# First attention layer: dense matmuls moved into the four gaps behind the attention products, turned inputs and values in one turn of a PSUM bank, two residual buffers

## The reference, cut to what matters

```
x = x + layernorm(attn(layernorm(x)))            # first layer
  attn(x): q, k, v = split(x @ w_qkv.T + b_qkv)  # x (16, 256, 128); 16 heads of 8
           a = softmax(q @ k.T / sqrt(128))      # per sequence and head, 256 x 256
           return (a @ v) @ w_o.T + b_o + x
x = x + layernorm(ffn(layernorm(x)))             # second attention, then 8 experts
```

## Time and profile before

| | us |
|---|---|
| median of 3 runs | 684.3 |
| lowest and highest | 680.41 and 688.04 |
| the profiled execution's own time | 679.28 |
| its span in the trace | 677.5 |
| mean granted TensorE clock over the span | 0.889 of 2.4 GHz |

### The profile page before, as it was taken

One profiled execution on the slowest core, in us unless ns is written; L12 is line 12 of the kernel. 1 busy time (PEld: TensorE's weight loads), 2 busy tenths in 40 slices (PEclk: granted clock), 3 DMA queues, 4 the chain that ended last, 5 costly groups with the idle time before them and its releaser, 6 DMA issues. The chain is left out here.

```text
span 677.5 us, 16101 instructions
## 1 busy us (share of the span) xinstructions
PE 552.5 (82%) x5228; PEld 415.3 (61%) x5228; DVE 455.5 (67%) x1285; ACT 373.1 (55%) x989; POOL 326.6 (48%) x543
## 2 busy tenths in 40 slices
PE   3899999999998988999991788897987409999920
PEld 2576566666665655565650677786876308999920
DVE  2366777787776667676853488888687633788870
ACT  0225666666665635665560498886774005677750
POOL 5142233334454345432114536775888750257776
PEclk9999999999998867998996699999876558999975
DMA  4200423110000000000011000000000122234333
GB/s 120 50 2 15 146 64 51 22 22 18 19 16 6 18 17 3 16 19 18 18 34 31 31 2 2 1 1 2 14 24 19 40 85 66 50 51 65 37 31 31
DMA packets 38099, 21.62 MB, mean 32 GB/s; under 512 B 13433, under 2 KB 36353, under 8 KB 38018
## 3 DMA queue, kind: packets, MB, share of 16 engines
q1 hardware_dynamic: 18544, 10.65, 7.0%
q0 software_dynamic: 6640, 4.92, 5.2%
q10 hardware_dynamic: 12834, 5.04, 3.0%
HBM read 10.11 MB, written 8.12 MB: 27 GB/s over the span
## 5 line engine op out<-in xcount | busy, mean ns | idle before, releaser
L330 DVE TENSOR_REDUCE nmax<-psA 128x2 f32<-128x512 f32 x256 | 165.3, 686 | 89.4 <-PE psA L209 89.0
L492 ACT ACTIVATE pr<-psB 128x512 f32<-128x512 f32 x250 | 136.0, 596 | 123.9 <-PE psB L226 121.4
L209 PE MATMUL psA<-km,qp 24*128 24x256 f32 x768 | 139.6, 446 | 1.0 <-POOL km L585 0.5
L226 PE MATMUL psB<-q,km 26*128 26x256 f32 (+1 forms) x752 | 118.9, 434 | 0.8 <-DMA q<-mT 0.8
L209 PEld LDWEIGHTS psA<-km,qp 24*128 24x128 f32 x768 | 91.0, 209 | 33.7 <-DVE nmax L330 23.2
L1601 POOL DMA_INDIRECT out<-wz,ys x39 | 63.5, 1627 | 53.2 <-ACT wz L1556 44.4
L585 POOL TENSOR_TENSOR km<-kraw,rows_of 128x768 f32<-128x768 f32 x16 | 23.5, 1467 | 127.7 <-ACT kraw L467 120.2
L226 PEld LDWEIGHTS psB<-q,km 26*128 26x128 f32 (+1 forms) x752 | 73.4, 202 | 1.8 <-DMA q<-mT 1.2
L240 PE MATMUL psO<-pr,v 128*32 128x256 f32 x1024 | 71.9, 401 | 0.1
L1164 ACT ACTIVATE prob<-psS,nbias 128x128 f32<-128x128 f32 x128 | 45.5, 380 | 10.4 <-DVE nbias L983 10.3
L240 PEld LDWEIGHTS psO<-pr,v 128*32 128x32 f32 x1024 | 27.5, 112 | 34.6 <-issue 23.3
(11 more groups left out here) (198 smaller groups left out, 1223.4 us busy)
## 6 DMA issues: line engine op xcount, KB each, us to landing
q<-mT SPq DMA_DIRECT2D x256, 1.0 KB
ys<-y_sorted SPq DMA_DIRECT2D x39, 72.0 KB, 1.9
e_w<-W ACTq DMA_DIRECT2D x1, 2048.0 KB
e_w<-W ACTq DMA_DIRECT2D x4, 512.0 KB
xs<-x_all SPq DMA_DIRECT2D x16, 128.0 KB
out<-x_all SPq DMA_DIRECT2D x15, 128.0 KB, 3.7
x_all<-x SPq DMA_DIRECT2D x1, 1536.0 KB, 9.1
out<-wz,ys POOLq DMA_INDIRECT x39, 3.4
```

The lines of the kernel that those rows point to most:

```text
L209: last = T.matmul(psA[:, (16 * b + n) % 3, c * L1:(c + 1) * L1], query_part(b, h, depth, c), keys(b, h, depth, slice(0, L1)), start=True, ...
L226: last = T.matmul(bank_of(b, h)[:, c * L1:(c + 1) * L1], keys(b, h, depth, slice(c * P, (c + 1) * P)), queries(b, h, depth, slice(0, L1)), ...
L330: V.tensor_reduce(nmax[:, b % 2, hf, :, at], psA[:, (16 * b + n) % 3, :].rearrange("p (c m) -> p c m", c=2), AX.X, ALU.max, negate=True).t ...
L492: A.activation(pr[:, h % PRING, :, :].rearrange("p c l -> p (c l)"), bank_of(b, h), ACT.Exp, scale=SCALE1).then_inc(S["b_free"], 1)
```

## The change

On TensorE `prep_x(i+2)` and `prep_v(i)` now follow each other in step 1, behind `attend`. `prep_qk` moves from steps 2 and 4 to 3 and 5 (behind `attend`), `project` from 6 to 7 (behind `attend`). So steps 0 and 1, 2 and 3, 4 and 5, 6 and 7 stand side by side without a full-array matmul between them. For most blocks the turned inputs of block i+2 and the values of block i share one turn of `misc` (left and right half), with one `full` and one `free`. The values are made in the block's own iteration, no longer in the one before.

`r1` has two buffers. `residual(b)` runs at the head of VectorE's iteration b+2, and waits only for the block before last on GpSimd; its statistics follow in step 1. `stats_x` moves to step 5, `normalise(i-1, 1)` to 3, `normalise(i, 0)` to 7 behind the last maxima. On ScalarE the turned inputs and the values are copied at the head of step 2, the queries at the head of 4, the keys at the head of 6, and the second order of the queries after the exponentials of step 7.

```diff
--- before.py
+++ after.py
@@ -76,7 +76,7 @@
         on = sb("on", [P, 8, 4, C1])
         onR = sb("onR", [P, L1])
         onT = sb("onT", [P, L1])
-        r1 = sb("r1", [P, 2, P])
+        r1 = sb("r1", [P, 2, 2, P])
         nr = sb("nr", [P, 2, P])
 
         psA = pb("psA", [P, 3, 512])
@@ -87,7 +87,7 @@
         names = ["ld_w", "ld_wo", "ld_b", "ld_v", "ld_x0", "ld_x1", "ld_x2", "ld_x3", "consts", "brow0", "w_zero",
                  "m_step", "w_ok", "stats0", "stats1", "aggr0", "aggr1", "ln0_step", "ln1_step", "xn_ok", "xnb_ok",
                  "full", "free", "q_ok", "k_ok", "km_ok", "v_ok", "v_zero", "a_full", "a_free",
-                 "turned", "norm_ok", "heads_ok", "onT_ok", "mrow0", "mrow1", "b_full", "b_free", "av_done", "o_ev", "rden_ok", "x1_ok", "stored",
+                 "turned", "norm_ok", "heads_ok", "onT_ok", "xnT_ok", "mrow0", "mrow1", "b_full", "b_free", "av_done", "o_ev", "rden_ok", "x1_ok", "stored",
                  "part_ok", "bias_ok"]
         S = {n: sem(n) for n in names}
 
@@ -98,6 +98,10 @@
 
             return 0 <= i + d <= LAST
 
+        def shares(b):
+
+            return 4 <= b <= LAST
+
         def piece(b):
             return next(k for k, (lo, hi) in enumerate(pieces) if lo <= b < hi)
 
@@ -105,7 +109,7 @@
 
         def turn(*name):
 
-            turns[name] = len(turns)
+            turns[name] = len(set(turns.values()))
 
         turn("w")
         turn("bias")
@@ -113,9 +117,11 @@
             for what in ("xT", "q", "k", "v"):
                 turn(what, b)
         for i in range(LAST + 2):
-            for what, b in (("xT", i + 2), ("q", i + 2), ("k", i + 2), ("out", i - 1), ("v", i + 1)):
+            for what, b in (("xT", i + 2), ("v", i), ("q", i + 2), ("k", i + 2), ("out", i - 1)):
                 if 0 <= b <= LAST and (what, b) not in turns:
                     turn(what, b)
+                if what == "v" and 2 <= i and i + 2 <= LAST:
+                    turns[("v", i)] = turns[("xT", i + 2)]
 
         def place(h):
 
@@ -174,7 +180,8 @@
                 pe.wait_ge(S["xn_ok"], b + 1)
                 for c in range(2):
                     last = T.transpose(misc[:, c * P:(c + 1) * P], xn[:, b % 2, c, :], ident[:, :])
-                last.then_inc(S["full"], 1)
+                if not shares(b):
+                    last.then_inc(S["full"], 1)
 
             def prep_qk(b, k, t):
                 if t == 0:
@@ -185,16 +192,16 @@
                 if t == 1:
                     made.then_inc(S["full"], 1)
 
-            def token_major(lhs, k):
-
-                for c in range(2):
-                    last = T.matmul(misc[:, c * P:(c + 1) * P], lhs[:, c * P:(c + 1) * P], wvo[:, k, :],
+            def token_major(lhs, k, half=0):
+
+                for c in range(2 * half, 2 * half + 2):
+                    last = T.matmul(misc[:, c * P:(c + 1) * P], lhs[:, c % 2 * P:(c % 2 + 1) * P], wvo[:, k, :],
                                     start=True, stop=True)
                 last.then_inc(S["full"], 1)
 
             def prep_v(b):
                 begin("v", b)
-                token_major(xnT[:, b % 2, :], 0)
+                token_major(xnT[:, b % 2, :], 0, int(shares(b + 2)))
 
             def scores_for_max(b, n):
 
@@ -265,13 +272,13 @@
                         attend(i - 1, 3)
                     if g == 1 and fits(i, 2):
                         prep_x(i + 2)
-                    if g in (2, 4) and fits(i, 2):
+                    if g == 1 and i >= 2 and here:
+                        prep_v(i)
+                    if g in (3, 5) and fits(i, 2):
                         prep_qk(i + 2, g // 2 - 1, 0)
                         prep_qk(i + 2, g // 2 - 1, 1)
-                    if g == 6 and done:
+                    if g == 7 and done:
                         project(i - 1)
-                    if g == 7 and i >= 1 and next_:
-                        prep_v(i + 1)
 
             pe.wait_ge(S["w_ok"], 5)
             prep_x(0)
@@ -313,13 +320,14 @@
             def residual(b):
                 dve.wait_ge(S["full"], turns[("out", b)] + 1)
                 dve.wait_ge(S["xnb_ok"], b + 1)
-                dve.wait_ge(S["x1_ok"], b)
-                V.tensor_tensor(out=r1[:, :, :], in0=misc[:, 0:2 * P].rearrange("p (c d) -> p c d", c=2),
+                dve.wait_ge(S["x1_ok"], count(b - 1))
+                V.tensor_tensor(out=r1[:, b % 2, :, :], in0=misc[:, 0:2 * P].rearrange("p (c d) -> p c d", c=2),
                                 in1=xnb_all[:, 2 * b:2 * b + 2, :], op=ALU.add).then_inc(S["free"], 1)
 
             def residual_stats(b):
                 dve.wait_ge(S["free"], turns[("out", b)] + 1)
-                ln_stats(1, b, r1, mv_r)
+                dve.wait_ge(S["x1_ok"], b)
+                ln_stats(1, b, r1[:, b % 2, :, :], mv_r)
 
             def maxima(b, n):
                 h = n ^ 2
@@ -365,6 +373,8 @@
             def iteration(i):
                 next_, done = fits(i, 1), fits(i, -1)
                 for g in range(8):
+                    if g == 0 and fits(i, -2):
+                        residual(i - 2)
                     if g == 2 and done:
                         turn_rows(i - 1, 1)
                     if g == 6 and fits(i, 0):
@@ -374,18 +384,15 @@
                         maxima(i + 1, 2 * g + 1)
                     if g in (3, 7) and next_:
                         turn_maxima(i + 1, g // 4)
-                    if g == 0 and fits(i, -2):
+                    if g == 1 and fits(i, -2):
                         residual_stats(i - 2)
-                    if g == 1 and fits(i, EARLY):
+                    if g == 5 and fits(i, EARLY):
                         stats_x(i + EARLY)
-                    if g == 2 and done:
+                    if g == 3 and done:
                         normalise(i - 1, 1)
-                    if g == 3 and done:
                         heads(i - 1)
-                    if g == 6 and fits(i, 0):
+                    if g == 7 and fits(i, 0):
                         normalise(i, 0)
-                    if g == 7 and done:
-                        residual(i - 1)
 
             stats_x(0)
             dve.wait_ge(S["w_zero"], 1)
@@ -438,7 +445,11 @@
                 if b >= 2:
                     ready("v", b - 2)
                 ready("xT", b)
-                A.activation(xnT[:, b % 2, :], misc[:, 0:L1], ACT.Copy).then_inc(S["free"], 1)
+                last = A.activation(xnT[:, b % 2, :], misc[:, 0:L1], ACT.Copy)
+                if shares(b):
+                    last.then_inc(S["xnT_ok"], 1)
+                else:
+                    last.then_inc(S["free"], 1)
 
             def queries_in(b):
                 ready("q", b)
@@ -472,8 +483,11 @@
             def values_in(b):
                 ready("v", b)
                 act.wait_ge(S["av_done"], count(4 * (b - SLOTS + 1)))
+                lo = L1 if shares(b + 2) else 0
+                if shares(b + 2):
+                    act.wait_ge(S["xnT_ok"], b + 2 - 3)
                 A.activation(v32[:, b % SLOTS, :, :, 0:C1],
-                             misc[:, 0:2 * P].rearrange("p (a h c) -> p a h c", a=2, c=C1),
+                             misc[:, lo:lo + L1].rearrange("p (a h c) -> p a h c", a=2, c=C1),
                              ACT.Copy).then_inc(S["free"], 1)
                 act.wait_ge(S["free"], turns[("v", b)] + 1)
                 act.sem_inc(S["v_ok"])
@@ -495,18 +509,18 @@
             def iteration(i):
                 here, next_, done = fits(i, 0), fits(i, 1), fits(i, -1)
                 for g in range(8):
-                    if g == 5 and fits(i, 2):
+                    if g == 2 and fits(i, 2):
+                        turned_x(i + 2)
+                    if g == 2 and i >= 2 and here:
+                        values_in(i)
+                    if g == 4 and fits(i, 2):
+                        queries_in(i + 2)
+                    if g == 6 and fits(i, 2):
                         keys_in(i + 2)
                     if here:
                         exponentials(i, 2 * g)
                         exponentials(i, 2 * g + 1)
-                    if g == 0 and i >= 2 and here:
-                        values_in(i)
-                    if g == 1 and fits(i, 2):
-                        turned_x(i + 2)
-                    if g == 3 and fits(i, 2):
-                        queries_in(i + 2)
-                    if g == 6 and fits(i, 2):
+                    if g == 7 and fits(i, 2):
                         queries_in_parts(i + 2)
                     if g == 5 and done:
                         heads(i - 1)
@@ -590,7 +604,7 @@
 
                 ln_scale(1, b, mv_r)
                 for c in range(2):
-                    last = G.tensor_scalar(nr[:, c, :], r1[:, c, :], nm[1][:, c:c + 1], rs[1][:, c:c + 1],
+                    last = G.tensor_scalar(nr[:, c, :], r1[:, b % 2, c, :], nm[1][:, c:c + 1], rs[1][:, c:c + 1],
                                            ALU.add, ALU.mult)
```

## The result

The kernel got slower by 1.0%: 689.8 us against 681.0 (medians of 20 runs each, 681.7 to 697.9 and 677.6 to 692.4), a ratio of 1.0104 [1.0072, 1.0136]. That ratio compares the executions of each kernel that lie within 1.5% of its fastest (17 and 16 of the 20); the quotient of the two medians is 1.013. Forecast was 685.5, a ratio of 1.0018. The profiled execution of the changed kernel has a span of 687.0 us at a granted clock of 0.913, that of before 677.5 at 0.889.

A forecast was written before the change was run, and what follows sets the result against it. TensorE's program was taken to set the pace. 17.5 (twelve blocks) + 2.2 (blocks 0, 1, 14, 15) - 19.3 (collision, low clock) = +0.4, or +2.0: middle 680.5, scaled by 1.0074 to 685.5 us; range 676 to 699.

The forecast's parts named there:

- The quiet block: Blocks 2 to 13 at full clock: 19.85 us each instead of 18.39, +17.5 for twelve.
- the wait for `qp`: PE at a block's end waits for ScalarE's second order of the queries: 0.17 to 0.28 us, taken as 0.21.
- the lost cover: Queries, keys and projection, nearly free between two steps, cost full length behind the product: +0.81, +0.75, +0.64 a block.
- The pair's wait: Two steps of scores side by side cost 3.00, not 2.20: 0.8 waiting for VectorE's maxima to free psA's three banks.
- "Much faster": Rival: the pair's wait comes from how steps happen to stand; four pairs cost 2.20 each, 645 us; chance 0.05.
- The collision: Blocks 8 to 10: VectorE's `on` runs beside POOL's bias sum, delaying the residual and PE; all 17.7 us forecast to go.
- signs of being right: Among them: `on` never over 0.5 and the clock 1.00 through blocks 8 to 11.
- a waiting `on` gets its turn between part and sum: In POOL's bias work, VectorE's `on` starts at the part's end, before the sum: a delay of 0.15, unseen by PE.
- the rival: Slower: `on` still falls into the bias sum, +3.9 or +15.9 with low clock; 689 to 701, middle 695; chance 0.23.
- The term that was mis-sized is the clock: Block 13's remaining 1.64 is a short 1.2 GHz stretch; between none and one such stretch stays, +0 to +1.6.
- a rival (every second block, +9 us, 694): Four pairs a block hold a 0.8 wait, so the clock falls more often, 1.64 every second block; chance 0.10.
- Blocks 0 and 1: Block 0 +1.56 for queries and keys; block 1 +1.03, less 0.75 of waiting for rows of maxima.

The follow-up runs named there:

- experiment 5: Changed kernel with ScalarE's second order of the queries ahead of the exponentials of step 7 instead of behind them; 682.7 us, ratio 0.9991 to the kernel before.
- Experiment 1: Changed kernel with queries, keys and projection put back between two steps of scores (steps 2, 4, 6), the rest kept; 651.4 us, ratio 0.9569 to the kernel before.
- experiments 8 and 9: Changed kernel with maxima and exponentials both halved, 663.3 us, ratio 0.9698; with only the maxima halved, 680.1 us, ratio 0.9977.
- Experiment 2: Kernel before with only `normalise(i, 0)` moved from step 6 to step 7, behind the residual; 667.5 us, ratio 0.9828.
- experiment 3: Changed kernel with `normalise` moved behind the next iteration's residual, where the bias sum runs; 693.8 us, ratio 1.0212 to the kernel before.
- experiment 6: The changed kernel run again unchanged, for a second profile; 690.7 us, span 688.9.
- Experiments 1 and 4: Experiment 1, and the changed kernel with transposes and values, queries, keys and projection all between two steps, residual back in step 7; the latter 642.4 us, ratio 0.9428.

## Why the prediction was right in its mechanism and where it was off

**The quiet block**: forecast 19.85, measured 19.81. Of the +1.42, queries and keys cost 1.06 each behind a product, values and transposes 0.81 together (forecast 0.36 + 0.43 = 0.79), the wait for `qp` 0.17 in the rows and 0.24 by experiment 5 (forecast 0.21). All pairs are 3.00. Experiment 1 prices the lost cover. The prediction's terms for it make 0.81 + 0.75 + 0.64 + 0.21 = 2.41; measured are 2.36 from block 8 on, and 2.06 ahead of it, where the moved statistics make the projection's pair 0.30 longer. The prediction put VectorE's moved work at nothing; that holds in the changed kernel, whose pairs are all 3.00 at full clock, and fails once a section stands in that pair.

**The pair's wait**: halving both readers takes 0.23 off a pair, halving the maxima alone 0.02 (experiments 8 and 9). It is the two rings of three banks waiting on both readers, where the prediction had the maxima alone. "Much faster" is out: no run had a pair near 2.20, the shortest is 2.77.

**The collision**: forecast gone, measured gone in full (-19.3 with block 13's; `on` at most 0.32 in blocks 8 to 10). Two of the prediction's signs of being right failed: `on` took 0.75 in block 11, and the clock was 0.96 over blocks 8 to 11, by the falls. `on` was asked for 0.24 before the sum, forecast 0.23. That a waiting `on` gets its turn between part and sum was never put to the test: it started 0.16 before the part's recorded end (231.30 against 231.46) and was not longer than elsewhere by more than 0.02. Experiment 2 shows the gain without the rest of the change, experiment 3 that the rival is real when `on` is issued inside the sum, and costs 2.4 and 3.95 with the low clock behind it, where the rival had 1.3 to 5.3 a block.

**The term that was mis-sized is the clock**, between none and one short stretch at 1.2 GHz, "+0 to +1.6". It measured 6 x 1.34 = 8.0. The prediction had this as a rival (every second block, +9 us, 694) and gave it 0.10; it came to pass beside the forecast mechanism, not instead of it. Its argument against was block 14 of before, whose bare pairs ran at a clock of 1.00. That was one block: in the changed kernel the falls come after a run of such blocks, and half of those have none. The matmul rows could not show it: 99% busy, largest idle time 0.17. What a row calls busy contains the pair's wait, since a pair is 3.00 of records for 2.20 of work.

**Blocks 0 and 1**: forecast +1.56 and +0.28 = +1.84, measured +2.86. But this stretch differs by 2.0 between two executions of the same kernel (experiment 6, 1.2 of it a fall in block 1), so the miss of 1.0 can't be read.

The sum by the prediction's way with the measured terms: 17.0 (12 x 1.42) + 2.9 + 8.0 - 19.3 = +8.6 to the last projection, against 8.5 read there; the remaining 1.0 of the span lies behind the layer and stays open.

**Luck.** The two large terms, +17.5 and -19.3, came out to within 0.5, and that is the mechanism. The final number is nearer than the sum: the profiled execution took 688.75 against a forecast of 680.5, 8.25 more, while the median is only 4.3 over 685.5. The forecast was scaled to a median of 684.3 from three executions, and twenty give 681.0; those 3.3 made the miss look smaller. By the prediction's own limits for no change, 677.5 and 691.1, the median of 689.8 is inside; the ratio's interval, 1.007 to 1.014, reaches to both sides of one per cent. "The gain and the loss cancel" is true of the two large terms and not of the kernel, which is slower.

## What to carry to other kernels

A section of matmuls costs what the next start says, not what its rows say: between two steps whose banks still wait for their readers it costs 0 to 0.3, behind work that nobody waits for its full 0.4 to 1.1. So gaps are no place for dense work when the steps themselves hold waits; put it inside the waits (here 0.94 of the time before, not 1.01). A change that mixes a good edit with bad ones should be taken apart: here one moved call alone gave 1.7%, the shared turn with its new order 0.64 to 0.94 us a block, and the regrouping took back more than both. And a wait that doesn't show in one version can show in the next: the moved statistics cost nothing until a section stood in their pair, then 0.30.

## What the hardware showed

The granted clock fell to 1.2 GHz from 168.3 to 171.6 in block 5, worth 1.34, and so at the same place of every second block, with no idle time over 0.17 us in the matmul rows ahead of it. The six falls came back in the same blocks in a second execution. They moved to every third block when the block was 0.21 longer, five of the six went when it was 0.28 shorter without more work in it, and all went at nearly equal length (19.86) when the pair's waits held work. Experiments 1 and 4 have no fall from block 2 to 13 either; their sections fill part of the same waits, which fits, but their blocks are also shorter, and the two weren't tried apart. What exactly the chip looks at stays open.

A VectorE instruction of 0.29 took 1.58 when it was issued 0.93 into GpSimd's sum of 2.35, and ended within 0.2 of it; issued 1.75 into one of 2.35 (block 11) it took 0.75 and ended 0.15 behind it; issued 0.24 before the sum it took 0.31.
